# Linear attention with keys and queries in turns, values last, elu split between ScalarE and one VectorE instruction, and the first low-part split on GpSimd

## The chip, the cores and the metric

The kernel runs on one core of one Trainium2 chip. The metric is the device time of the whole program in microseconds. A core has TensorE (PE), VectorE (DVE), ScalarE (ACT), GpSimd (POOL), a queue that issues most transfers (SP) and 16 DMA engines.

## The reference, cut to what matters

Two layers of a perceiver-like network on x of shape (2, 128, 512): each a cross attention, an attention and a feed-forward block. The change is in the second layer's attention and at the start of its feed-forward:

```python
x = x + _L1_attn_ref(_layernorm(x), ...)      # linear attention
x = x + _L1_ffn_ref(_layernorm(x), ...)       # gated, two hidden layers of 2048
# _L1_attn_ref
fmap = lambda t: jax.nn.elu(t) + 1.0
Q = fmap(x @ Wq + bq);  K = fmap(x @ Wk + bk);  value = x @ Wv + bv
KV = jnp.sum(K * value, axis=1);  Ksum = jnp.sum(K, axis=1)
Z = 1.0 / (Q * Ksum[:, None, :] + 1e-06)
V = Q * KV[:, None, :] * Z
out = jax.nn.gelu(V @ Wo + bo)
```

## The kernel before

The program is written engine by engine: `linear_pe`, `linear_act`, `linear_dve` are what TensorE, ScalarE and VectorE do in linear attention, `ffn_pe`, `ffn_scalar`, `ffn_dve` the same for the feed-forward. Each engine takes its instructions in the order in which they are written; between engines stand semaphores, and `link` makes VectorE wait for its own last instruction, `link_a` ScalarE. No planner reorders anything.

T = 256 is both batches' 128 positions side by side, and C = 4 is the number of chunks of 128 of the width 512. Projections are in fp32 and leave `[128 columns of the width, 256 positions]` in PSUM, four accumulated matmuls for a column chunk; they read the normalised, transposed input `xnT`. Weights come in blocks of 128x2048 (1 MB) through a ring of four buffers: block k goes into buffer k % 4, and SP issues it when `blk_used` says that block k - 4 is used up. The blocks of linear attention are K, V, Q and the output projection, in that order in memory; the first feed-forward block takes the buffer of K.

Before: TensorE projects keys, values and queries, one matrix after the other (L2063). VectorE adds the bias to each piece into `lz` (L2095 for keys and values, L2113 for queries), takes the minimum with 0 (L2099, L2114), ScalarE takes the exponential (L2078, L2081), and VectorE adds max(lz, 0) (L2101, L2122). Sums over a batch's positions are reductions (L2103, L2106). For queries it goes on chunk by chunk: denominators (L2126), their reciprocal (L2128), the product `lvT` (L2131), and `lv_ready` lets TensorE do two output matmuls of 512 columns (L2070). Then bias (L2138), gelu on ScalarE (L2085), residual (L2142), statistics for the next layer normalisation (L244 to L252).

The feed-forward multiplies in three passes of a faster number format: each operand is split into a high part, which ScalarE makes by a cast (`split_hi`, L2181; `norm_hi` for the input), and a low part, which VectorE makes by subtracting (`split_lo`, L2186; L2282 for the input). `w_hi` and `w_lo` count split weight blocks. TensorE starts when block 0 and both parts of the input are there (L2215). Where TensorE has to wait it does filler matmuls, `keep_clock` (L279).

GpSimd makes one low part in the first layer (L2401, 128x1024), issues the transfers of the context, and is free after 1050 us.

Of the kernel before, what the change touches and what calls it, by code (L numbers as in the profile page):

```python
# [16 lines left out]
P = 128  # L17
B = 2
D = 512
C = D // P  # L20
T = B * P
# [12 lines left out]
RING = 4  # L34
# [7 lines left out]
BLK_LIN = BLK_X1 + 2  # L42
# [73 lines left out]
def build(nc, x, ctxT, ctx_rows, wq, wk, wv, wo, stream, small, cols, rows, consts, out):  # L116
# [6 lines left out]
    with ExitStack() as ctx:  # L123
# [1911 lines left out]
        lz = view(0, 3, C, T)  # L2035
# [3 lines left out]
        lden = view(8 * C * T, C * B, P)  # L2039
# [5 lines left out]
        LIN_Q_BANK = (2, 3, 4, 5)  # L2045
        lin_filled = sem("lin_filled")
        lmin_ready = sem("lmin_ready")
        lexp_ready = sem("lexp_ready")
        lv_ready = sem("lv_ready")
# [3 lines left out]
        def linear_pe(pe):  # L2053

            norm_pe(pe, 4)
            for m in range(3):
                need(pe, BLK_LIN + m)
                for cc in range(C):
                    out = psum[:, LIN_Q_BANK[cc], 0:T] if m == 2 else psum[:, 4 + 2 * m + cc // 2, (cc % 2) * T:(cc % 2) * T + T]
                    if m == 2 and cc == 2:  # L2060
                        pe.wait_ge(lexp_ready, 1)
                    for c in range(C):
                        last = nc.tensor.matmul(out, block(BLK_LIN + m)[:, c, cc * P:(cc + 1) * P], xnT[:, c, :],  # L2063
                                                start=c == 0, stop=c == C - 1)
                    last.then_inc(lin_filled if cc < C - 1 else blk_used, 1)
            need(pe, BLK_LIN + 3)
            for c in range(C):
                pe.wait_ge(lv_ready, c + 1)
                for b in range(B):
                    last = nc.tensor.matmul(psum[:, b, :], lvT[:, c, b * P:(b + 1) * P], block(BLK_LIN + 3)[:, c, :],  # L2070
                                            start=c == 0, stop=c == C - 1)
                    if c == C - 1:
                        last.then_inc(lin_filled if b == 0 else blk_used, 1)

        def linear_act(act):
            norm_act(act, 4)
            act.wait_ge(lmin_ready, 1)
            nc.scalar.activation(le[:, 0, :, :], le[:, 0, :, :], ACT.Exp).then_inc(lexp_ready, 1)  # L2078
            for cc in range(C):
                act.wait_ge(lmin_ready, cc + 2)  # L2080
                nc.scalar.activation(le[:, 1, cc, :], le[:, 1, cc, :], ACT.Exp).then_inc(lexp_ready, 1)  # L2081
# [5 lines left out]
        def linear_dve(dve):  # L2087
            norm_dve(dve, 4)
            for m in range(2):
                for cc in range(C):  # L2090
# [422 lines left out]
```

## Time and profile before

| | |
|---|---|
| median of 3 runs | 1392.0 us (1389.58, 1392.0, 1392.38) |
| profiled execution | 1391.61 us, span 1389.8 us |
| TensorE busy, mean granted clock | 1319.1 us (95%), 0.978 |
| weight loads busy | 1127.0 us (81%) |
| VectorE busy | 901.5 us (65%) |
| ScalarE busy | 684.6 us (49%) |
| GpSimd busy | 12.0 us (1%) |
| chain that ended last | PE 84%, DVE 10%, issue 3%, ACT 2%, DMA 1% |

The span is the time from the first to the last instruction; the profiled execution's own time is 1.8 us more. Busy shares are of the span. The chain names, at each moment, the work for which everything after it had to wait; an engine's busy time outside the chain costs nothing. A PE row in a timeline counts two records for an fp32 matmul.

### The profile page before, as it was taken

What the parts mean: (1) busy time and instruction counts of PE and PEld (TensorE: products, weight loads), DVE (VectorE), ACT (ScalarE), POOL (GpSimd) and SP (SyncE); (2) the same over time, 40 slices, a digit from 0 to 9 for tenths busy, and PEclk for the clock granted to TensorE, in tenths of its full rate; (3) what the DMA queues carried; (4) which work ended last, traced back from release to release, by engine and by line L of the source; (5) the groups of instructions that cost most, each with busy time, mean ns of one, the idle gap of its engine ahead of it and who ended that gap; (6) DMA issues with size and microseconds to landing.
All of it is one profiled execution on the core that took longest, in us unless ns stands there. A gap on an engine that the chain in (4) does not pass through costs nothing.

```text
span 1389.8 us, 23595 instructions
## 1 busy us (share of the span) xinstructions
PE 1319.1 (95%) x9874; PEld 1127.0 (81%) x9874; DVE 901.5 (65%) x1163; ACT 684.6 (49%) x815; POOL 12.0 (1%) x18
## 2 busy tenths in 40 slices
PE   7999999989999999896899999999899889999998
PEld 6899899979999997665677777777654679999997
DVE  3666565766665666687678888888616667444443
ACT  4534444454444443561377777777404144555442
POOL 0000000000000000000000000000100000000000
PEclk9999999999999999985899999999999999999999
DMA  7101011301010021210079998999840325455552
GB/s 281 40 23 44 20 35 54 127 15 43 20 35 20 21 76 47 92 62 33 31 277 338 342 345 338 343 346 355 331 170 8 121 91 182 172 184 183 185 182 77
DMA packets 50220, 197.67 MB, mean 142 GB/s; under 512 B 12112, under 2 KB 20560, under 8 KB 30416
## 3 DMA queue, kind: packets, MB, share of 16 engines
q1 hardware_dynamic: 47792, 187.41, 37.3%
q0 software_dynamic: 2336, 8.91, 1.9%
q8 instruction: 72, 1.18, 0.3%
q14 instruction: 20, 0.16, 0.0%
HBM read 195.78 MB, written 0.52 MB: 141 GB/s over the span
## 4 chain that ended last, share of the span: by engine, by line
PE 84%; DVE 10%; issue 3%; ACT 2%; DMA 1%; SPq 0%; POOL 0%; POOLq 0%; DVEq 0%; ACTq 0%
PE psum L453 13%; PE psum L2233 13%; PE psum L428 13%; PE psum L1538 8%; PE psum L480 5%; PE psum L1558 4%; PE psum L505 4%; PE psum L1541 4%; PE psum L2215 3%; PE psum L1561 2%; PE psum L2246 2%; PE psum L2063 1%; PE psum L464 1%; PE psum L1570 1%; PE psum L1837 1%
## 5 line engine op out<-in xcount | busy, mean ns | idle before, releaser
L1599 DVE TENSOR_TENSOR arena_r<-ring,arena_r 128x2048 fp32r<-128x2048 f32 x96 | 219.6, 2290 | 36.4 <-ACT arena_r L1593 36.1
L453 PE MATMUL psum<-ring_r,arena_r 128*128 128x256 f32 x1536 | 201.4, 289 | 3.5 <-ACT arena_r L723 2.5
L453 PEld LDWEIGHTS psum<-ring_r,arena_r 128*128 128x128 f32 x1536 | 192.0, 194 | 4.2 <-issue 2.7
L428 PE MATMUL psum<-arena_r 128*128 128x512 f32 x768 | 186.0, 397 | 9.8 <-ACT arena_r L757 9.6
L1593 ACT CAST arena_r<-ring 128x2048 fp32r<-128x2048 f32 x96 | 183.4, 1913 | 17.1 <-PE psum L1541 10.7
L2233 PE MATMUL psum<-arena_r 128*128 128x256 f32 x1536 | 184.6, 283 | 1.1 <-DVE arena_r L2292 1.1
L2233 PEld LDWEIGHTS psum<-arena_r 128*128 128x128 f32 x1536 | 184.4, 192 | 1.3 <-issue 1.3
L428 PEld LDWEIGHTS psum<-arena_r 128*128 128x128 f32 x768 | 143.1, 190 | 42.1 <-issue 8.4
L2186 DVE TENSOR_TENSOR arena_r<-ring,arena_r 128x2048 fp32r<-128x2048 f32 x44 | 100.8, 2292 | 117.0 <-ACT arena_r L2181 117.0
L2181 ACT CAST arena_r<-ring 128x2048 fp32r<-128x2048 f32 x44 | 83.6, 1901 | 111.2 <-PE psum L2233 85.3
L1538 PE MATMUL psum<-arena_r 128*128 128x512 f32 x512 | 132.5, 401 | 1.3 <-issue 1.3
L1538 PEld LDWEIGHTS psum<-arena_r 128*128 128x128 f32 x512 | 94.2, 188 | 23.2 <-issue 5.0
L744 ACT COPY arena<-psum 128x1024 f32<-128x1024 f32 x64 | 61.7, 1016 | 89.6 <-PE psum L480 89.6
L616 DVE TENSOR_TENSOR arena<-arena,psum 128x1024 f32<-128x1024 f32 x64 | 75.2, 1216 | 28.0 <-PE psum L494 28.0
L301 DVE TENSOR_TENSOR arena_r<-arena,arena_r 128x768 fp32r<-128x768 f32 (+2 forms) x25 | 33.7, 1353 | 74.9 <-ACT arena_r L715 57.1
L736 ACT COPY ring<-psum 128x512 f32<-128x512 f32 x64 | 37.3, 582 | 87.0 <-PE psum L453 87.0
L751 ACT ACTIVATE arena<-arena 128x1024 f32<-128x1024 f32 x64 | 66.2, 1058 | 19.8 <-DVE arena L616 18.5
L596 DVE TENSOR_TENSOR arena<-arena 128x512 f32<-128x512 f32 (+1 forms) x128 | 71.5, 559 | 4.4
L1541 PE MATMUL psum<-arena_r 128*128 128x512 f32 x256 | 68.6, 390 | 0.0
L480 PEld LDWEIGHTS psum<-qT,arena 64*128 64x128 f32 x1024 | 59.7, 188 | 9.9 <-issue 9.1
L480 PE MATMUL psum<-qT,arena 64*128 64x128 f32 x1024 | 65.8, 278 | 0.8 <-issue 0.8
L1558 PE MATMUL psum<-arena_r 128*128 128x512 f32 x256 | 64.2, 393 | 0.5 <-DVE arena_r L1767 0.5
(314 smaller groups left out, 1686.3 us busy)
## 6 DMA issues: line engine op xcount, KB each, us to landing
ring<-in_stream SPq DMA_DIRECT2D x151, 1024.0 KB, 4.8
arena<-in_ctxT POOLq DMA_DIRECT2D x8, 1024.0 KB, 11.9
arena<-in_ctxT SPq DMA_DIRECT2D x7, 1024.0 KB, 8.0
arena<-in_wk SPq DMA_DIRECT2D x16, 256.0 KB, 3.2
wv_in<-in_wv SPq DMA_DIRECT2D x8, 512.0 KB, 3.4
arena<-in_wq SPq DMA_DIRECT2D x16, 256.0 KB, 2.6
arena<-in_wk SPq DMA_DIRECT2D x16, 128.0 KB, 3.1
arena<-in_wo SPq DMA_DIRECT2D x2, 1024.0 KB, 6.3
```

Of the source, the lines that this page charges most:

```text
L428: last = nc.tensor.matmul(bank, wk_sb[wp][:, c, w], cx[xp][kb][:, c, :], start=c == wp == xp == 0, stop=c == C - 1 and xp == 1)
L453: last = nc.tensor.matmul(bank[:, q * T:(q + 1) * T], cx[xp][kc // 4][:, c, kc % 4 * P:(kc % 4 + 1) * P], wv_sb[wp][:, c, :], start=c == w ...
L480: last = nc.tensor.matmul(psum[:, 2 * half + kc // 4, kc % 4 * P:kc % 4 * P + P], kT[j % 2][a:a + 64, k0:k0 + P], qT[a:a + 64, j % 2, half ...
L616: nc.vector.tensor_tensor(part, part, per_row(psum[:, SPREAD_BANK, 0:P], KC // 2), ALU.subtract).then_inc(shifted, 1)
L1538: nc.tensor.matmul(out, xg[xp][:, c, e, :], hi[:, c, :], start=c == xp == 0, stop=False)
L1541: last = nc.tensor.matmul(out, xg[0][:, c, e, :], lo[:, c, :], start=False, stop=c == C - 1)
L1558: nc.tensor.matmul(psum[:, 5, :], hT[u][hp][:, f, :], hi[:, f, :], start=u == f == hp == 0, stop=False)
L1593: nc.scalar.copy(mwhi[p % MB], ring[k % RING][:, :]).then_inc(moe_hi, 1)
L1599: nc.vector.tensor_tensor(mwlo[p % MB], ring[(BLK_MOE + p) % RING][:, :], mwhi[p % MB].bitcast(fp32), ALU.subtract).then_inc(moe_lo if p < ...
L2181: nc.scalar.copy(whi[j % 2], ring[k % RING][:, :]).then_inc(w_hi, 1)
L2186: nc.vector.tensor_tensor(wlo[j % 2], ring[(BLK_W12 + j) % RING][:, :], whi[j % 2].bitcast(fp32), ALU.subtract).then_inc(w_lo, 1)
L2233: last = nc.tensor.matmul(psum[:, 4 + s, 0:T], w[wp][:, c, :], src[xp][:, c, :], start=c == wp == xp == 0, stop=c == FC - 1 and wp == 1)
```

## The change

It does these things:

- Keys and queries are projected in turns, piece by piece, and values last; each piece has a PSUM bank of its own, and V takes the banks of K (`lk_ready` says that VectorE has read one).
- 1 + elu(z + b) is written as max(z + b + 1, exp(-relu(-(z + b)))). ScalarE does the relu out of PSUM (L2097) and the exponential (L2099), VectorE one instruction (L2114), which for keys also gives the sum over positions as its accumulator output (`lks`). Key times value is one instruction with `lkvs` as accumulator output (L2135). The bias constants `lone` and `lneg` are made ahead of the layer normalisation.
- Denominators and reciprocals of all chunks come before the values.
- The low part of the first feed-forward block is made by GpSimd; the split of the second comes behind the input's parts on ScalarE and VectorE.
- The residual of batch 0 no longer waits behind a split, and its statistics come right behind it.
- The first buffers of the ring are given free by the first matmul of a later matrix; the count of `blk_used` stays the same at the end.
- Filler ahead of the feed-forward is 10 and 3 matmuls instead of 13 and 4.

```diff
-        def norm_stats_dve(dve, n):
-            for b in range(B):
+        def norm_stats_dve(dve, n, batches=range(B)):
+            for b in batches:
                 ins = nc.vector.bn_stats(stats[:, b, :], x_res[:, b, :])
...
+        LIN_BLK = {"k": BLK_LIN, "v": BLK_LIN + 1, "q": BLK_LIN + 2}
+        LIN_BANK = {"k": (4, 5, 6, 7), "v": (4, 5, 6, 7), "q": (2, 3, 0, 1)}
+        LIN_BIAS = {"k": 0, "v": C, "q": 2 * C}
...
         def linear_pe(pe):
 
             norm_pe(pe, 4)
...
+            def project(m, cc, first_done=0):
+                for c in range(C):
+                    last = nc.tensor.matmul(psum[:, LIN_BANK[m][cc], 0:T], block(LIN_BLK[m])[:, c, cc * P:(cc + 1) * P], xnT[:, c, :],
+                                            start=c == 0, stop=c == C - 1)
+                    if c == 0 and first_done:
+                        last.then_inc(blk_used, first_done)
+                last.then_inc(lin_filled, 1)
+
+            need(pe, LIN_BLK["k"])
+            need(pe, LIN_BLK["q"])
+            for cc in range(C):
+                project("k", cc)
+                project("q", cc)
+            need(pe, LIN_BLK["v"])
+            for cc in range(C):
+                pe.wait_ge(lk_ready, cc + 1)
+                project("v", cc, 1 if cc == 0 else 0)
             need(pe, BLK_LIN + 3)
             for c in range(C):
                 pe.wait_ge(lv_ready, c + 1)
                 for b in range(B):
-                    last = nc.tensor.matmul(psum[:, b, :], lvT[:, c, b * P:(b + 1) * P], block(BLK_LIN + 3)[:, c, :],
+                    last = nc.tensor.matmul(psum[:, 2 + b, :], lvT[:, c, b * P:(b + 1) * P], block(BLK_LIN + 3)[:, c, :],
                                             start=c == 0, stop=c == C - 1)
+                    if c == b == 0:
+                        last.then_inc(blk_used, 2)
...
         def linear_act(act):
             norm_act(act, 4)
...
+            for n in range(2 * C):
+                cc, i, m = n // 2, n % 2, "kq"[n % 2]
+                act.wait_ge(lin_filled, n + 1)
+                col_ = LIN_BIAS[m] + cc
+                link_a(act, nc.scalar.activation(le[:, i, cc, :], psum[:, LIN_BANK[m][cc], 0:T], ACT.Relu,
+                                                 bias=lneg[:, col_:col_ + 1], scale=-1.0))
+                nc.scalar.activation(le[:, i, cc, :], le[:, i, cc, :], ACT.Exp, scale=-1.0).then_inc(lexp_ready, 1)
             split_hi(act, 0)
...
         def linear_dve(dve):
+            nc.vector.tensor_scalar(lone[:, :], K_("lin_b", 0, 3 * C), 1.0, None, ALU.add)
+            link(dve, nc.vector.tensor_scalar(lneg[:, :], K_("lin_b", 0, 3 * C), -1.0, None, ALU.mult))
             norm_dve(dve, 4)
+            halves = [slice(b * P, (b + 1) * P) for b in range(B)]
+            def one_plus_elu(m, cc, t, **kw):
+                i, col_ = "kq".index(m), LIN_BIAS[m] + cc
+                return nc.vector.scalar_tensor_tensor(lqk[:, i, cc, t], psum[:, LIN_BANK[m][cc], t], lone[:, col_:col_ + 1],
+                                                      le[:, i, cc, t], ALU.add, ALU.max, **kw)
+            for cc in range(C):
+                dve.wait_ge(lexp_ready, 2 * cc + 1)
+                for b, t in enumerate(halves):
+                    ins = one_plus_elu("k", cc, t, accum_out=lks[:, cc * B + b:cc * B + b + 1])
+                ins.then_inc(lk_ready, 1)
+                dve.wait_ge(lexp_ready, 2 * cc + 2)
+                link(dve, one_plus_elu("q", cc, slice(0, T)))
+                for b, t in enumerate(halves):
+                    i = cc * B + b
+                    ins = nc.vector.tensor_scalar(lden[:, cc, t], lqk[:, 1, cc, t], lks[:, i:i + 1], 1e-6, ALU.mult, ALU.add)
                 link(dve, ins)
...
+                ins = nc.vector.reciprocal(lden[:, cc, :], lden[:, cc, :])
+            link(dve, ins)
             for cc in range(C):
...
+                dve.wait_ge(lin_filled, 2 * C + cc + 1)
+                col_ = LIN_BIAS["v"] + cc
+                for b, t in enumerate(halves):
+                    i = cc * B + b
+                    ins = nc.vector.scalar_tensor_tensor(lkv[:, i, :], psum[:, LIN_BANK["v"][cc], t], K_("lin_b", col_), lqk[:, 0, cc, t],
+                                                         ALU.add, ALU.mult, accum_out=lkvs[:, i:i + 1])
                 link(dve, ins)
...
+                    ins = nc.vector.scalar_tensor_tensor(lvT[:, cc, t], lqk[:, 1, cc, t], lkvs[:, i:i + 1], lden[:, cc, t],
+                                                         ALU.mult, ALU.mult)
                 ins.then_inc(lv_ready, 1)
...
-            split_lo(dve, 0)
             for b in range(B):
                 dve.wait_ge(lgelu, b + 1)
-                ins = nc.vector.tensor_tensor(x_res[:, b, :], x_res[:, b, :], ly[:, b, :], ALU.add)
-            link(dve, ins)
+                link(dve, nc.vector.tensor_tensor(x_res[:, b, :], x_res[:, b, :], ly[:, b, :], ALU.add))
+                if b == 0:
+                    nc.vector.bn_stats(stats[:, b, :], x_res[:, b, :])
...
         def ffn_pe(pe):
-            keep_clock(pe, 6, 13)
+            keep_clock(pe, 6, 10)
...
-            keep_clock(pe, 6, 4)
+            keep_clock(pe, 6, 3)
...
         def ffn_scalar(act):
             norm_std_act(act, 5)
-            split_hi(act, 1)
             for b in range(B):
                 act.wait_ge(xnT_filled, 2 * 5 + b + 1)
                 nc.scalar.copy(fxT[0][:, :, b * P:(b + 1) * P], psum[:, b, :].rearrange("p (c t) -> p c t", c=C)).then_inc(norm_hi, 1)
+            split_hi(act, 1)
...
         def ffn_dve(dve):
-            norm_stats_dve(dve, 5)
-            split_lo(dve, 1)
+            norm_stats_dve(dve, 5, (1,))
...
+            dve.wait_ge(w_lo, 1)
+            split_lo(dve, 1)
...
+            gp.wait_ge(w_hi, 1)
+            nc.gpsimd.tensor_tensor(wlo[0], ring[BLK_W12 % RING][:, :], whi[0].bitcast(fp32), ALU.subtract).then_inc(w_lo, 1)
```

On ScalarE, at the start of linear attention behind the transposed input's copy (`xnT`), the order is now as follows; `arena` is the memory of `le`:

```order
 L273 COPY xnT<-psum 128x4x128 [waits xnT_filled]
-L2078 ACT_TABLE_LOAD
-L2078 ACTIVATE arena<-arena 128x1024 [waits lmin_ready]
-L2081 ACTIVATE arena<-arena 128x256 [waits lmin_ready] x4
-L2181 CAST arena_r<-ring 128x2048 [waits blk_arrived3]
-L2085 ACT_TABLE_LOAD
-L2085 ACTIVATE arena<-arena 128x512 [waits ly_ready] x2
+L2097 ACTIVATE arena<-psum,lneg 128x256 [waits lin_filled]
+L2099 ACT_TABLE_LOAD
+L2099 ACTIVATE arena<-arena 128x256 [waits a_chain]
+L2097 ACTIVATE arena<-psum,lneg 128x256 [waits lin_filled]
+L2099 ACTIVATE arena<-arena 128x256 [waits a_chain]
```

The exponential's table load has moved from in front of all activations to behind the first relu, and each piece now has two activations of 256 columns.

On VectorE, at the values, one chunk of the program after the change is this (`arena` holds `lkv`, `lqk`, `lden` and `lvT`):

```order
+L2135 SCALAR_TENSOR_TENSOR arena,lkvs<-psum,col,arena 128x128 [waits lin_filled]
+L2135 SCALAR_TENSOR_TENSOR arena,lkvs<-psum,col,arena 128x128
+L2140 SCALAR_TENSOR_TENSOR arena<-arena,lkvs 128x128 [waits v_chain]
+L2140 SCALAR_TENSOR_TENSOR arena<-arena,lkvs 128x128
+L2148 TENSOR_TENSOR arena<-psum,row 128x512 [waits lin_filled]
+L2148 TENSOR_TENSOR arena<-psum,row 128x512 [waits blk_used]
+L2151 TENSOR_TENSOR x_res<-x_res,arena 128x512 [waits lgelu]
+L2153 BN_STATS stats<-x_res 128x6 [waits v_chain]
+L2151 TENSOR_TENSOR x_res<-x_res,arena 128x512 [waits lgelu]
 L244 BN_STATS stats<-x_res 128x6 [waits v_chain]
```

Between an output projection's chunk and the one before it stand now four short instructions, no reciprocal; and between the bias additions (L2148) and the residual (L2151) no split any more.

On GpSimd, at the end of its program:

```order
+L2419 DMA arena<-in_ctxT 128x4x512 x5
+L2422 DMA arena<-in_ctx_rows,pick 128x512 [waits picked] x2
+L2425 TENSOR_TENSOR arena_r<-ring,arena_r 128x2048 [waits w_hi]
 L123 UNCONDITIONAL_BRANCH
```

The subtraction is its last instruction and waits for ScalarE's high part alone.

## Rows read from the trace of the kernel before

**Rows 1.** Windows, linear attention's second half; busy us (instructions) of each engine, clock, DMA

```profile
1104.30:1119.10 14.80, 7.96 (x18) 3.09 (x18) 12.99 (x27) 4.04 (x5) 0.00 (x0) 1.00 0.21 71
```

**Rows 2.** Chain that ended last, 1060 to 1150: start us, us, what

```profile
1083.36 17.52 PE psum L2063 x80
...
1103.29 1.76 DVE arena L2128
```

**Rows 3.** Timeline of PE: start us, us, line, what, count, idle before

```profile
1083.36 20.96 PE L2063 MATMUL psum<-xnT,ring 128*128 128x256 f32 x96 [0.72 <-DVE xnT L261]
1105.84 1.95 PE L2070 MATMUL psum<-ring,arena 128*128 128x512 f32 x4 [1.53 <-DVE arena L2131]
...
1117.07 1.98 PE L2070 MATMUL psum<-ring,arena 128*128 128x512 f32 x4 [1.31 <-DVE arena L2131]
1118.89 5.78 PE L279 MATMUL psum<-cst 128*128 128x256 f32 x26
1125.96 1.11 PE L2199 MATMUL psum<-cst,xn 128*128 128x128 f32 x8 [1.29 <-DVE xn L252]
...
1130.54 46.30 PE L2215 MATMUL psum<-arena_r 128*128 128x256 f32 x384 [1.74 <-issue]
```

**Rows 4.** Timeline of DVE, 1068 to 1150

```profile
1102.77 0.48 DVE L2126 TENSOR_SCALAR arena<-arena,lks 128x128 f32<-128x128 f32 x2
...
1105.08 0.61 DVE L2131 SCALAR_TENSOR_TENSOR arena<-arena,lkvs 128x128 f32<-128x128 f32 x2
...
1119.09 0.69 DVE L2138 TENSOR_TENSOR arena<-psum,row 128x512 f32<-128x512 f32 x1 [0.17 <-PE psum L2070]
1119.70 2.28 DVE L2186 TENSOR_TENSOR arena_r<-ring,arena_r 128x2048 fp32r<-128x2048 f32 x1
1121.90 1.29 DVE L2142 TENSOR_TENSOR x_res<-x_res,arena 128x512 f32<-128x512 f32 x2
1123.22 1.29 DVE L244 BATCH_NORM_STATS2 stats<-x_res 128x6 f32<-128x512 f32 x2
...
1126.94 2.29 DVE L2186 TENSOR_TENSOR arena_r<-ring,arena_r 128x2048 fp32r<-128x2048 f32 x1 [0.58 <-ACT arena_r L2181]
1129.15 1.28 DVE L2282 TENSOR_TENSOR arena_r<-psum,arena_r 128x512 fp32r<-128x512 f32 x2
```

**Rows 5.** Timeline of ACT, 1068 to 1150

```profile
1083.27 1.28 ACT L2078 ACT_TABLE_LOAD   x1
...
1101.72 0.42 ACT L2081 ACTIVATE arena<-arena 128x256 f32<-128x256 f32 x1 [8.48 <-DVE arena L2114]
...
1110.79 1.88 ACT L2181 CAST arena_r<-ring 128x2048 fp32r<-128x2048 f32 x1
...
1119.82 0.63 ACT L2085 ACTIVATE arena<-arena 128x512 f32<-128x512 f32 x1 [0.23 <-DVE arena L2138]
```

**Rows 6.** Groups of instructions by line: busy us, mean ns of one, idle before

```profile
L2289 DVE SCALAR_TENSOR_TENSOR arena<-psum,col,arena 128x256 f32<-128x256 f32 x16 | 7.7, 478 | 3.7 <-ACT arena L2262 3.7
...
L2262 ACT ACTIVATE arena<-psum,col 128x256 f32<-128x256 f32 x16 | 7.5, 470 | 8.4 <-PE psum L2215 8.4
```

**Rows 7.** Timeline of ACT in the second cross attention, accumulator reads

```profile
1050.45 0.19 ACT L1941 ACTIVATION_READ_ACCUMULATOR arena<-psum,nlm 128x1 f32 x1
1050.54 0.36 ACT L1941 ACTIVATE arena<-psum,nlm 128x128 f32<-128x128 f32 x1
```

**Rows 8.** Timeline of all engines, 681.7 to 686

```profile
681.78 2.41 POOL L2401 TENSOR_TENSOR arena_r<-xn,arena_r 128x1024 fp32r<-128x1024 f32 x1 [112.17 <-ACT arena_r L1607]
...
683.43 0.80 DVE L1664 TENSOR_TENSOR gt_rank<-sc,gm 128x16 f32<-128x16 f32 x1
...
685.30 0.18 DVE L1664 TENSOR_TENSOR gt_rank<-gt_rest,gm 128x16 f32<-128x16 f32 x1
```

**Rows 9.** DMA issues of L222 between 1085 and 1100

```profile
DMA to landing us min/median/max: 4.8/4.8/4.9
```

**Rows 10.** Windows, 630 to 642, columns as in rows 1

```profile
630.00:642.00 12.00, 4.64 (x72) 4.08 (x76) 11.04 (x17) 1.58 (x4) 0.00 (x0) 0.55 0.18 72
```

More of the change, by code:

```diff
@@ L2032, in cross1_dve @@
             link(dve, nc.vector.tensor_tensor(x_res[:, 1, :], x_res[:, 1, :], psum[:, X1_BANK[1], :], ALU.add))
-        lz = view(0, 3, C, T)
         le = view(3 * C * T, 2, C, T)
@@ L2038, in build @@
         lkv = view(7 * C * T, C * B, P)
-        lden = view(8 * C * T, C * B, P)
+        lden = view(8 * C * T, C, T)
         lvT = view(9 * C * T, C, T)
@@ L2043, in build @@
         lks = sb("lks", [P, C * B])
-        LIN_Q_BANK = (2, 3, 4, 5)
+        lneg = sb("lneg", [P, 3 * C])
+        lone = sb("lone", [P, 3 * C])
+        LIN_BLK = {"k": BLK_LIN, "v": BLK_LIN + 1, "q": BLK_LIN + 2}
+        LIN_BANK = {"k": (4, 5, 6, 7), "v": (4, 5, 6, 7), "q": (2, 3, 0, 1)}
+        LIN_BIAS = {"k": 0, "v": C, "q": 2 * C}
         lin_filled = sem("lin_filled")
-        lmin_ready = sem("lmin_ready")
         lexp_ready = sem("lexp_ready")
+        lk_ready = sem("lk_ready")
         lv_ready = sem("lv_ready")
@@ L2055, in linear_pe @@
             norm_pe(pe, 4)
[L2056 to L2065, printed above, removed]
+            def project(m, cc, first_done=0):
[14 more added lines that the diff above has]
+                project("v", cc, 1 if cc == 0 else 0)
             need(pe, BLK_LIN + 3)
@@ L2116, in linear_dve @@
-            query_in(0)
-            for cc in range(C):
-                if cc + 1 < C:
-                    query_in(cc + 1)
-                dve.wait_ge(lexp_ready, cc + 2)
-                q = lqk[:, 1, cc, :]
-                link(dve, nc.vector.scalar_tensor_tensor(q, lz[:, 2, cc, :], 0.0, le[:, 1, cc, :], ALU.max, ALU.add))
-                den = lden.rearrange("p (c b) t -> p c (b t)", c=C)[:, cc, :]
-                for b in range(B):
-                    i, t = cc * B + b, slice(b * P, (b + 1) * P)
-                    ins = nc.vector.tensor_scalar(den[:, t], q[:, t], lks[:, i:i + 1], 1e-6, ALU.mult, ALU.add)
+            halves = [slice(b * P, (b + 1) * P) for b in range(B)]
@@ L2129, in linear_dve @@
-                for b in range(B):
-                    i, t = cc * B + b, slice(b * P, (b + 1) * P)
-                    ins = nc.vector.scalar_tensor_tensor(lvT[:, cc, t], q[:, t], lkvs[:, i:i + 1], den[:, t], ALU.mult, ALU.mult)
+                for b, t in enumerate(halves):
+                    i = cc * B + b
+                    ins = nc.vector.scalar_tensor_tensor(lvT[:, cc, t], lqk[:, 1, cc, t], lkvs[:, i:i + 1], lden[:, cc, t],
+                                                         ALU.mult, ALU.mult)
```

34 lines of the change are left out of this document (2 added, 32 removed).

## The prediction

> **What bounds the kernel now.** I read the table of windows first, then the chain of work that ended last, then the timelines of the engines around linear attention. TensorE is busy for 95% of the span (the table above), so an edit pays only where TensorE has nothing to do, or does filler. Between the last projection and the end of the output projection there is such a place: TensorE is busy 7.96 of 14.80 us, VectorE 12.99 [rows 1]. The chain says who ends last: it runs in TensorE for 17.52 us of projections, and then in VectorE, whose reciprocals of 1.76 us are on it four times [rows 2]. TensorE's timeline shows the same from its side: projections for 20.96 us, then four groups of output matmuls, the first at 1105.84 and the last at 1117.07, with idle time between them; then filler, the transposes at 1125.96, filler, and the first feed-forward matmul at 1130.54 [rows 3]. VectorE's timeline fills the last stretch [rows 4]: after the second bias addition (1119.09) a low-part split of 2.28 us, only then the residual (1121.90) and the statistics, later a second split of 2.29 us in front of the two low parts of the normalised input (1129.15), whose end at 1130.43 releases the feed-forward. From 1130.54 on nothing in the chain is touched by the change. So two stretches can be won: the projections to the end of the output projection, and from there to 1130.54.
>
> I count t from the first projection matmul (1083.36). Before, the last output group starts at t = 33.7 and ends at about 35.7; the feed-forward starts at 47.2.
>
> **Ahead of t = 0.** `lone` and `lneg` stand between the residual and the statistics. They are two tiny instructions, and the statistics wait for the second; the smallest two-input instruction takes 0.18 us [rows 8], so the pair is between 0.2 and 0.4. I take 0.3 us, lost: nothing hides it.
>
> **Projections.** Twelve of them take 20.96 us, 1.73 each once the drain of the last is left out. The order becomes k q k q k q k q v v v v, with the same work. K and Q are done at t = 13.9, V at 20.8 if no wait for `lk_ready` bites.
>
> ScalarE per piece: one activation out of PSUM, 0.47 [rows 6], an estimated 0.13 for the wait between the two (0.05 to 0.3 changes nothing), and an exponential of 0.42 [rows 5], 1.02 together, against 1.73 between pieces, so it keeps up. The table load of 1.28 that was hidden in idle time [rows 5] now stands behind the first relu; the first pair is late by it (keys at 4.2, queries at 5.1), and it is never repeated.
>
> VectorE per column chunk: two halves of 1+elu for keys, one whole for queries 0.48 [rows 6], two denominators 0.48, a reciprocal 1.75 [rows 2, 4]. The keys' halves carry an accumulator output, which no instruction of VectorE has before. Bounds: without it a pair out of SBUF takes 0.61 [rows 4], some 0.68 out of PSUM; on ScalarE the accumulator read starts the next instruction 0.09 later [rows 7]; at worst each read costs as much as a smallest instruction on its own, 0.2 to 0.3. I take 0.88 a pair, as its nearest relative on ScalarE says, range 0.68 to 1.3. A chunk is then 0.88+0.51+0.52+1.75 = 3.6, against 3.46 of two projections: nearly balanced. From 5.1 for the first query: first reciprocal done at 8.0, the fourth at 18.8. `lk_ready` comes at 5.1, 8.8, 12.5 and 16.1, always ahead of V's need (13.9, 15.6, 17.3, 19.1).
>
> Values: an accumulating pair (0.9) and the scaled pair (0.61), 1.5 per chunk: `lv_ready` at 20.3, 21.8, 23.3, 24.7. The output projection has the columns of four projections, so unhindered it goes 20.8 to 27.7, and wants them at 20.8, 22.5, 24.3 and 26.0. TensorE would bound it: 8.0 us earlier than before's 35.7.
>
> **GpSimd's split.** The buffer of the K block is now given free at V's first matmul, t = 14.4, instead of about 7.0. A block lands 4.8 us after its issue [rows 9], with 0.4 for the queue: 19.6. ScalarE's half takes 1.88 [rows 5], to 21.5. GpSimd then subtracts 2048 columns. Its one row with half of them says 2.41, so 4.8: 21.6 to 26.4. That is far ahead of the feed-forward's need. But it isn't free. During the 2.41 us of GpSimd's subtraction before, VectorE's L1664 with two SBUF inputs took 0.80 us, ending just when GpSimd was done (684.23 against 684.19); the same instruction 1.9 us later takes 0.18 [rows 8]. So VectorE's instructions with two SBUF inputs stand still until GpSimd ends. Those are the scaled pairs (`lqk`, `lden`). The second one ends at 21.8, about when GpSimd starts; I take it that it slips through. The third, due at 22.7, is held to 26.4: `lv_ready` 3 at 27.0 instead of 23.3. TensorE, which wanted it at 24.3, loses 2.8; the fourth comes at 28.5, in time for 28.8. The output projection ends at 30.5: 5.2 earlier than before, not 8.0.
>
> The Trainium skill, in SBUF — State Buffer, "Who interferes with whom", states it as a lock: a VectorE instruction with two SBUF inputs and a GpSimd one that reads SBUF exclude each other, for a whole instruction. The trace agrees with its 0.80 against 0.18. By its GPSIMD Engine Reference, "3.1 Elementwise", a 2048-column fp32 addition is 4.50 us on GpSimd; by that figure the loss would be an estimated 2.5.
>
> **From there to the feed-forward.** The split of 2.28 leaves VectorE. The second gelu ends at 1120.45 [rows 5]; the residual of batch 0 starts behind the second bias addition, at 1119.8 in old time, its statistics, the other residual and its statistics follow: four times 0.65 to 0.7, to 1122.5, where it was 1124.51 [rows 4]. Saved 2.0. Then the second split: ScalarE copies the transposed input first (0.58 each), VectorE subtracts behind each copy and no longer behind 2.29 of split. The chain is transposes, copy, subtract 0.68 for batch 1: the feed-forward starts 1.95 sooner still. Together 3.95. The split of block 1 lies behind, beside the first 48 feed-forward matmuls, 5.8 us (46.30 for 384) [rows 3]: 1.88 and 2.29 one after the other end 3.6 us after its start. If that cover were gone it would cost up to 4.2. The filler, 10 and 3 instead of 13 and 4, shrinks by 1.8 and stays shorter than the waits that it fills; it costs nothing.
>
> **The sum.** −5.2 + 0.3 − 3.95 = −8.85. The profiled execution took 1391.61, so 1382.8; the median of the runs shown is 0.4 above it, so 1383.0. What a measurement of this kernel tells from no change is about 0.2%, 2.8 us.
>
> **The rivals.**
> *No collision* (26%): GpSimd starts later or shorter than I think, or an operand in PSUM leaves the interface free. Speaks for it: half a microsecond decides. Sum −8.0+0.3−3.95 = −11.65: 1380.1.
> *The collision one chunk sooner* (17%): GpSimd gets in between the halves of the second scaled pair. `lv_ready` 2 at 27.0 against 22.5: 4.5 lost instead of 2.8, 1384.8.
> *Accumulating is dear* (8%): 1.3 a pair makes a chunk 4.1, so the fourth reciprocal ends at 20.2, the first scaled pair already meets GpSimd, and `lv_ready` is 1.95 apart from 27.0 on: the end at 34.6, 1387.2. The Trainium skill, in ScalarE: Activation LUTs, "Rules for kernel authors", would keep relu on VectorE; here that would put another 0.48 a piece on the engine that the chain runs in, and no run here shows it.
> *The split on the wrong side of the clock* (2%), the slower one: TensorE waits 2.8 us for the third scaled pair with no filler. In another stretch, where it was busy 4.64 of 12 us, the granted clock fell to 0.55 [rows 10], between its two levels 1.2 and 2.4 GHz. At 1.2 GHz the busy time doubles. To lose the 8.85 and 2.8 more it takes 23 us at the lower level. Against it: gaps of 1.53 and 1.31 us and two more ahead of these same matmuls left the clock at 1.00 [rows 1, 3]. Over 1395.
> *The change is hidden* (2%): something else, a late block 1 say, holds the feed-forward; about 1390.
> My forecast has 45%.
>
> **The numbers.** 1383.0. No collision and 1384.8 are inside; a dearer accumulator reaches 1386.5, and with the spread of the runs the lower bound is 1379.3. Faster 0.95, same 0.03, slower 0.02.
>
> **What would show it.** A table load once, behind the first relu. TensorE without gaps over the twelve projections. The output projection's first matmul 20.8 us after the first projection's. A scaled pair on VectorE of over 3 us that ends with GpSimd's instruction, and as long a gap in TensorE. The feed-forward 7.5 us after the output projection's end, where it was 11.5. Wrong would make it: `lk_ready` as what V waits for, a w_hi or w_lo wait of TensorE at the third pair of feed-forward columns, or a granted clock under 1.00 between t = 20 and 50.

## The result, and the profile after

The changed kernel takes 1378.91 us, the median of 6 runs (1376.2 to 1383.62), against 1390.0 for the kernel before (6 runs, 1387.96 to 1392.38). The ratio is 0.9907, with a 95% interval of 0.9888 to 0.9926. Measured a second time it is 0.9916 (0.9889 to 0.9943). It is faster, by a little less than 1%, and both intervals leave out 1. 1383.0 was predicted, with 1379.3 to 1386.5 as the range: the gain is larger than forecast, and the first median lies 0.4 us below the range. The second, 1379.71 from 10 runs, lies inside it, so what was wrong has to be read from the trace and not from the whole time.

The head of the page of the changed kernel:

```profile
span 1375.0 us, 23605 instructions
...
PE 1313.6 (96%) x9866; PEld 1123.1 (82%) x9866; DVE 896.1 (65%) x1175; ACT 688.9 (50%) x826; POOL 16.5 (1%) x19
```

The spans of the two profiled executions differ by 14.8 us, but that is not the change alone. What runs before t = 0 is the same code but for the 0.3 us of `lone` and `lneg`, and it took 1083.36 us in one execution and 1079.79 in the other. In the thirteen profiles of this study the first projection matmul starts between 1079.79 and 1090.05. So I compare from there on, in t, as the prediction did. The timeline of PE, which answers to [rows 3]:

```profile
1079.79 20.96 PE L2065 MATMUL psum<-xnT,ring 128*128 128x256 f32 x96 [0.72 <-DVE xnT L261]
1100.59 5.31 PE L2084 MATMUL psum<-ring,arena 128*128 128x512 f32 x12
1106.15 1.98 PE L2084 MATMUL psum<-ring,arena 128*128 128x512 f32 x4 [0.26 <-DVE arena L2140]
...
1112.96 1.11 PE L2209 MATMUL psum<-cst,xn 128*128 128x128 f32 x8 [0.51 <-DVE xn L252]
...
1115.66 46.31 PE L2225 MATMUL psum<-arena_r 128*128 128x256 f32 x384 [0.29 <-issue]
```

Three groups of output matmuls are one row now, without a gap; the fourth waits for 0.26 us for a scaled pair (L2140). The output projection ends at t = 28.3 (35.7 before), the feed-forward starts at t = 35.87 (47.18 before). The residual of batch 1 starts 5.57 us ahead of t = 0 instead of 5.30. Together −11.31 + 0.27 = −11.04 us.

The timeline of DVE, which answers to [rows 4]. First the second half of a key pair beside the read of the first half, and the chunk's reciprocal, then the last reciprocal, values and scaled pairs, then the tail:

```profile
1090.88 0.08 DVE L2114 DVE_READ_ACCUMULATOR arena<-psum,lone,arena 128x1 f32 x1
1090.88 0.35 DVE L2114 SCALAR_TENSOR_TENSOR arena<-psum,lone,arena 128x128 f32<-128x128 f32 x1
...
1092.42 1.75 DVE L2128 RECIPROCAL arena<-arena 128x256 f32<-128x256 f32 x1
...
1095.87 1.75 DVE L2128 RECIPROCAL arena<-arena 128x256 f32<-128x256 f32 x1
1097.66 0.35 DVE L2135 SCALAR_TENSOR_TENSOR arena<-psum,col,arena 128x128 f32<-128x128 f32 x1
...
1098.33 0.61 DVE L2140 SCALAR_TENSOR_TENSOR arena<-arena,lkvs 128x128 f32<-128x128 f32 x2
...
1100.71 0.61 DVE L2140 SCALAR_TENSOR_TENSOR arena<-arena,lkvs 128x128 f32<-128x128 f32 x2
1101.24 0.35 DVE L2135 SCALAR_TENSOR_TENSOR arena<-psum,col,arena 128x128 f32<-128x128 f32 x1
...
1101.90 4.20 DVE L2140 SCALAR_TENSOR_TENSOR arena<-arena,lkvs 128x128 f32<-128x128 f32 x2
...
1108.78 0.68 DVE L2151 TENSOR_TENSOR x_res<-x_res,arena 128x512 f32<-128x512 f32 x1
1109.50 0.69 DVE L2153 BATCH_NORM_STATS2 stats<-x_res 128x6 f32<-128x512 f32 x1
1110.11 0.68 DVE L2151 TENSOR_TENSOR x_res<-x_res,arena 128x512 f32<-128x512 f32 x1
1110.82 0.69 DVE L244 BATCH_NORM_STATS2 stats<-x_res 128x6 f32<-128x512 f32 x1
...
1114.27 1.29 DVE L2291 TENSOR_TENSOR arena_r<-psum,arena_r 128x512 fp32r<-128x512 f32 x2 [0.91 <-ACT arena_r L2265]
```

The first three scaled pairs take 0.61 us each, the third (1100.71) with GpSimd's instruction starting 0.46 us after it (1101.17, below), and the last one takes 4.20. The accumulator read is a record of its own (0.08), and the second half starts in the same moment as the read of the first. The residual and the statistics follow the bias addition with nothing between. The timeline of ACT:

```profile
1081.79 0.47 ACT L2097 ACTIVATE arena<-psum,lneg 128x256 f32<-128x256 f32 x1 [2.10 <-PE psum L2065]
1082.29 1.28 ACT L2099 ACT_TABLE_LOAD   x1
...
1090.43 0.47 ACT L2097 ACTIVATE arena<-psum,lneg 128x256 f32<-128x256 f32 x1 [0.80 <-PE psum L2065]
1090.93 0.42 ACT L2099 ACTIVATE arena<-arena 128x256 f32<-128x256 f32 x1
...
1099.19 1.90 ACT L2191 CAST arena_r<-ring 128x2048 fp32r<-128x2048 f32 x1 [4.39 <-DMA ring<-in_stream]
```

Timeline of POOL, the same kernel:

```profile
1101.17 4.52 POOL L2425 TENSOR_TENSOR arena_r<-ring,arena_r 128x2048 fp32r<-128x2048 f32 x1 [53.45 <-ACT arena_r L2191]
```

One table load, behind the first relu; a piece takes ScalarE 0.92 us (1090.43 to 1091.35). ScalarE's half of the split ends at t = 21.3, GpSimd subtracts from 21.4 to 25.9, and the long pair runs from 22.1 to 26.3. The chain of work that ended last, at the same place:

```profile
1079.79 14.07 PE psum L2065 x64
...
1101.90 4.21 DVE arena L2140 x2
```

### The profile page after: what moved, and what is told of

Its sections match the earlier page's. It is cut to its first block, busy times and chain, and to the rows that moved or that the text cites. A ratio compares the mean times of both kernels' runs of the same rounds, so it can differ in the third digit from the quotient of the medians.

```text
span 1375.0 us, 23605 instructions
## 1 busy us (share of the span) xinstructions
PE 1313.6 (96%) x9866; PEld 1123.1 (82%) x9866; DVE 896.1 (65%) x1175; ACT 688.9 (50%) x826; POOL 16.5 (1%) x19
## 4 chain that ended last, share of the span: by engine, by line
PE 86%; DVE 9%; ACT 2%; DMA 2%; issue 1%; SPq 0%; DVEq 0%; ACTq 0%
PE psum L2243 13%; PE psum L453 13%; PE psum L428 13%; PE psum L1538 8%; PE psum L480 5%; PE psum L1558 4%; PE psum L505 4%; PE psum L1541 4%; PE psum L2225 3%; PE psum L1561 2%; PE psum L2256 2%; PE psum L1837 2%; PE psum L464 1%; PE psum L1570 1%; PE psum L2065 1%
```

## The experiments

All were read in t, from the first projection matmul, because the stages ahead of it vary by more than the effects. What every profile gave, one execution each:

| kernel | t = 0 is at | output projection ends, t | feed-forward starts, t |
|---|---|---|---|
| before | 1083.36 | 35.69 | 47.18 |
| changed | 1079.79 | 28.34 | 35.87 |
| GpSimd's split alone | 1085.73 | 39.64 | 49.18 |
| split of block 1 behind, alone | 1090.05 | 35.69 | 45.30 |
| linear attention alone | 1082.18 | 27.83 | 39.31 |
| changed, profiled a second time | 1083.94 | 28.35 | 35.88 |
| changed, GpSimd after the pairs | 1082.38 | 27.82 | 35.35 |
| changed, GpSimd 1.7 us sooner | 1088.30 | 30.01 | 37.54 |
| the same, in four instructions | 1083.48 | 28.70 | 36.22 |
| changed, values 1.2 us later | 1083.08 | 30.13 | 37.66 |
| changed, no accumulator output | 1084.71 | 28.68 | 36.21 |
| changed, no filler | 1084.39 | 28.35 | 36.60 |
| changed, GpSimd after the pairs, constants early | 1083.53 | 27.83 | 35.35 |

The changed kernel's two profiles agree within 0.01 us in both columns, though their t = 0 lie 4.15 us apart. Five of the versions were timed once only: GpSimd sooner 1386.93 us, in four instructions 1380.82, values later 1381.83, no accumulator output 1382.01, no filler 1383.87. Runs of one kernel lie up to 14 us apart here (17 runs of the kernel before: 1386.16 to 1400.63), so these five times show nothing by themselves, and only the stage in the trace is read.

**My theory** was the prediction's own: the terms add up, GpSimd's instruction holds VectorE's instructions with two SBUF inputs, and only the place where it meets them was wrong. **The rival**: the long pair has another cause, GpSimd costs nothing, and the miss is in another term.

**GpSimd's split alone**, on the kernel before:

```diff
-            split_lo(dve, 0)                     # linear_dve
+            dve.wait_ge(w_lo, 1)                 # ffn_dve, ahead of split_lo(dve, 1)
+            gp.wait_ge(w_hi, 1)
+            nc.gpsimd.tensor_tensor(wlo[0], ring[BLK_W12 % RING][:, :], whi[0].bitcast(fp32), ALU.subtract).then_inc(w_lo, 1)
```

> The kernel before with one edit: the low part of the first feed-forward block is made by GpSimd, nothing else. Counted from the first projection matmul, the last output group starts at 33.7 us and the feed-forward at 47.2 us in the kernel before. Lock theory (a VectorE instruction with two SBUF inputs stands still while GpSimd subtracts): ScalarE's half ends where it ended before, GpSimd subtracts for 4.5 us from about 29.3 on, the third scaled pair (0.61 us) becomes a wait of over 3 us, the last output group starts at about 37.3, and the split of 2.3 us that leaves the path later does not pay for it: feed-forward at about 48.6, 1.4 us later than before. Rival (the long pair in the changed kernel had another cause, GpSimd is free): last group at 33.7, feed-forward at 45.0, 2.2 us earlier.

Timeline of DVE, the same kernel:

```profile
1115.47 4.55 DVE L2131 SCALAR_TENSOR_TENSOR arena<-arena,lkvs 128x128 f32<-128x128 f32 x2
```

Timeline of POOL, the same kernel:

```profile
1115.12 4.49 POOL L2414 TENSOR_TENSOR arena_r<-ring,arena_r 128x2048 fp32r<-128x2048 f32 x1 [62.90 <-ACT arena_r L2180]
```

Timeline of PE, the same kernel:

```profile
1120.08 5.29 PE L2070 MATMUL psum<-ring,arena 128*128 128x512 f32 x8 [5.07 <-DVE arena L2131]
...
1134.91 46.30 PE L2214 MATMUL psum<-arena_r 128*128 128x256 f32 x384 [1.32 <-issue]
```

The same pair that took 0.61 us takes 4.55 as soon as GpSimd subtracts beside it, and TensorE waits 5.07 us for it, where it waited 2.03 for that pair before. The feed-forward starts 2.0 us later than before, although a split of 2.3 us has left VectorE. In time: 1393.21 against 1391.04, ratio 1.0012 (0.999 to 1.0035), which is no difference that a measurement of whole times can tell; the trace can. The lock theory had it at 48.6, it is 49.18; the rival said 45.0. A side effect is seen in the windows (length, busy us of the engines, granted clock, DMA):

```profile
1113.00:1115.00 2.00, 2.00 (x3) 0.34 (x1) 1.93 (x4) 2.00 (x2) 0.00 (x0) 0.52 0.00 0
...
1123.00:1125.00 2.00, 2.00 (x6) 0.89 (x5) 0.76 (x3) 0.00 (x0) 0.00 (x0) 0.92 0.00 0
```

The clock was at its lower level already before the long wait, at output matmuls that ran at 1.00 in the kernel before with the same gaps ahead of them, and it stayed there until 1123. In the output projection this cost next to nothing: the last output group ends 2.67 us after its scaled pair starts (1122.70 to 1125.37), and did so 2.65 us after it in the kernel before (1116.40 to 1119.05). So the wait for the held pair is what ends the output projection 3.95 us later (t = 39.64 instead of 35.69), and 1.95 of it come back behind it, where the split of 2.3 us is gone.

**The split of block 1 behind the input's parts, alone**, on the kernel before:

```diff
             norm_std_act(act, 5)                 # ffn_scalar
-            split_hi(act, 1)
             for b in range(B): ...               # the input's high parts
+            split_hi(act, 1)
-            split_lo(dve, 1)                     # ffn_dve, the same
             for b in range(B): ...
+            split_lo(dve, 1)
```

> The kernel before with one edit: the split of the second feed-forward block comes behind the input's parts on ScalarE and VectorE. My sum's term: last output group unchanged at 33.7, feed-forward at 45.2 instead of 47.2. Rival (block 1 is then late for the third pair of feed-forward columns): the same start, but a gap in TensorE some 5.8 us behind it, and no gain in all.

Timeline of PE, the same kernel:

```profile
1135.35 46.30 PE L2215 MATMUL psum<-arena_r 128*128 128x256 f32 x384
```

Feed-forward at t = 45.30, 1.88 sooner (1.95 predicted), and its 384 matmuls take the same 46.30 us as in [rows 3]: block 1 is not late. In time the ratio is 1.0001 (0.9983 to 1.002): 1.88 us are 0.14%, inside that interval.

**Linear attention alone**, on the changed kernel:

```diff
-            gp.wait_ge(w_hi, 1)
-            nc.gpsimd.tensor_tensor(wlo[0], ...)
+            split_lo(dve, 0)                     # linear_dve, as before
                                                  # residual, statistics, split of block 1, filler: as before
```

> The changed linear attention alone: both splits, the residual, the statistics and the filler are as in the kernel before, and GpSimd does nothing here. The terms add up: last output group at 26.0 us from the first projection matmul (33.7 before, 26.4 in the changed kernel with GpSimd's collision), feed-forward 13.5 later at 39.5: some 7.4 us of the changed kernel's 11. Rival (linear attention's part is worth less by itself, because the tail needs the early buffers): feed-forward later than 40.5.

Timeline of PE, the same kernel:

```profile
1102.98 7.03 PE L2084 MATMUL psum<-ring,arena 128*128 128x512 f32 x16
```

All sixteen records of the output projection are one row of 7.03 us: without GpSimd TensorE never waits there. It ends at 27.83, 7.86 us sooner than before, and the feed-forward starts 7.87 sooner. In time 1384.14, ratio 0.995 (0.9931 to 0.997): −6.9 us between the medians, where the trace has −7.87 + 0.27.

**GpSimd after the scaled pairs**, on the changed kernel:

```diff
+            gp.wait_ge(lv_ready, C)
             gp.wait_ge(w_hi, 1)
```

> The changed kernel with one edit: GpSimd also waits until all four scaled pairs are done. Lock theory: the fourth scaled pair takes 0.6 us instead of 4.2 and ends at 22.8 us; the last output group starts at 26.0 instead of 26.4, so 0.3 us are won and no more, because TensorE is the bound there; GpSimd ends at 27.4, before VectorE's residual, and the feed-forward starts at 35.5 instead of 35.9. Rival (the pair is long for another reason): it stays at 4.2.

Timeline of DVE, the same kernel:

```profile
1104.49 0.61 DVE L2140 SCALAR_TENSOR_TENSOR arena<-arena,lkvs 128x128 f32<-128x128 f32 x2
```

Timeline of POOL, the same kernel:

```profile
1105.20 4.51 POOL L2426 TENSOR_TENSOR arena_r<-ring,arena_r 128x2048 fp32r<-128x2048 f32 x1 [54.93 <-DVE arena L2140]
```

The fourth pair is back at 0.61 us, and the feed-forward starts at 35.35: the collision cost the changed kernel 0.5 us. I had said 0.3 to 0.4. In time 1377.85, ratio 0.9913 (0.9891 to 0.9935), not to be told from the changed kernel.

**GpSimd 1.7 us sooner**, on the changed kernel:

```diff
-                project("q", cc)
+                project("q", cc, 1 if cc == C - 1 else 0)
...
-                project("v", cc, 1 if cc == 0 else 0)
+                project("v", cc)
```

> The changed kernel with one edit: the buffer of the K block is given free by the first matmul of the last query piece, 1.7 us sooner. Everything that GpSimd does is then 1.7 us sooner: 19.7 to 24.2 us from the first projection matmul. Lock theory: the second scaled pair, which starts at 19.7, or the third at 20.9 is held until 24.2. If the second: lv_ready 2 at 24.6 where TensorE wants it at 22.5, 2.0 us lost, last output group at 28.0 instead of 26.4. If the third: lv_ready 3 at 24.8, wanted at 24.3, 0.5 lost, last group at 26.5. A collision one chunk sooner is then dearer although nothing else changed. Rival (no lock): last group at 26.4 or 26.0 and no long pair at the place where GpSimd works.

Timeline of DVE, the same kernel:

```profile
1108.03 4.81 DVE L2140 SCALAR_TENSOR_TENSOR arena<-arena,lkvs 128x128 f32<-128x128 f32 x2
```

Timeline of POOL, the same kernel:

```profile
1107.93 4.50 POOL L2425 TENSOR_TENSOR arena_r<-ring,arena_r 128x2048 fp32r<-128x2048 f32 x1 [51.93 <-ACT arena_r L2191]
```

Timeline of PE, the same kernel:

```profile
1112.89 5.42 PE L2084 MATMUL psum<-ring,arena 128*128 128x512 f32 x12 [1.92 <-DVE arena L2140]
```

GpSimd had begun 0.1 us before the second pair's turn, and that pair takes 4.81 us; the second output group starts at t = 24.59, where I had put 24.6. TensorE waits 1.92 us, and the feed-forward starts at 37.54, 1.67 later than in the changed kernel. By its trace, a buffer that is free sooner made this stage slower.

**The same in four instructions**, so that VectorE may get a turn in between:

```diff
-            nc.gpsimd.tensor_tensor(wlo[0], ring[BLK_W12 % RING][:, :], whi[0].bitcast(fp32), ALU.subtract).then_inc(w_lo, 1)
+            for h in range(4):
+                s = slice(h * BLK // 4, (h + 1) * BLK // 4)
+                ins = nc.gpsimd.tensor_tensor(wlo[0][:, s], ring[BLK_W12 % RING][:, s], whi[0][:, s].bitcast(fp32), ALU.subtract)
+            ins.then_inc(w_lo, 1)
```

> As the run with the earlier buffer, and GpSimd subtracts in four instructions of 512 columns instead of one of 2048. If the interface is held for a whole instruction and then given up, a held pair waits for at most a quarter, some 1.2 us, and VectorE and GpSimd take turns: no pair over 2 us, last output group at 26.0 to 26.3. If VectorE stands still as long as GpSimd has anything to do, the picture is that of the run with one instruction.

Timeline of DVE, the same kernel:

```profile
1103.21 2.66 DVE L2140 SCALAR_TENSOR_TENSOR arena<-arena,lkvs 128x128 f32<-128x128 f32 x2
...
1106.45 1.97 DVE L2140 SCALAR_TENSOR_TENSOR arena<-arena,lkvs 128x128 f32<-128x128 f32 x2
```

Timeline of POOL, the same kernel:

```profile
1103.19 5.08 POOL L2427 TENSOR_TENSOR arena_r<-ring,arena_r 128x512 fp32r<-128x512 f32 x4 [52.00 <-ACT arena_r L2191]
```

The first half of the second pair by itself (the other takes 1.35):

```profile
1103.21 1.39 DVE L2140 SCALAR_TENSOR_TENSOR arena<-arena,lkvs 128x128 f32<-128x128 f32 x1
```

The two engines take turns, instruction by instruction: a quarter on GpSimd (some 1.3 us), half a pair, the next quarter, the other half. Two pairs are held, by 2.05 and 1.36 us, instead of one by 4.2. My "no pair over 2 us" was wrong, since a pair is two instructions and each can meet a quarter of its own. The last output group starts at 26.7, not at 26.0 to 26.3. The feed-forward starts at 36.22 instead of 37.54: most of the loss is gone, and 0.9 us against the version without a collision are left.

**Values 1.2 us later**, on the changed kernel:

```diff
             link(dve, ins)                       # the reciprocals
+            link(dve, nc.vector.reduce_sum(lkvs[:, 0:C], lqk[:, 0, :, :], AX.X))
```

> The changed kernel with one more reduction of 1.2 us on VectorE (one SBUF input, its result is overwritten) between the reciprocals and the values. It sets VectorE about as late as my prediction had it, with GpSimd where it was: 21.4 to 25.9 us from the first projection matmul. My prediction's price for the third scaled pair, redone with the measured 1.2 a chunk: the pair that was due at 22.1 is held to 25.9, lv_ready 3 at 26.5 where TensorE wants it at 24.3, last output group at 28.3 instead of 26.4, feed-forward at 37.8 instead of 35.9: 1.9 lost to a delay of 1.2. If instead the loss is VectorE's delay alone: the last group's wait grows from 0.26 to at most 1.5, last group below 27.6.

Timeline of DVE, the same kernel:

```profile
1105.26 4.20 DVE L2141 SCALAR_TENSOR_TENSOR arena<-arena,lkvs 128x128 f32<-128x128 f32 x2
```

Timeline of PE, the same kernel:

```profile
1109.51 3.70 PE L2084 MATMUL psum<-ring,arena 128*128 128x512 f32 x8 [2.04 <-DVE arena L2141]
```

This is the case of my prediction, made on purpose: the third pair is the long one, TensorE waits 2.04 us, and the feed-forward starts at 37.66 (37.8 expected), 1.8 us later for 1.2 us of work. Against the version without a collision (35.35) the third pair's collision costs 2.3 us, where I had 2.8 with longer chunks.

**No accumulator output**, on the changed kernel (the sums over positions are left out and stand at 1.0):

```diff
+            nc.vector.memset(lks[:, :], 1.0)
+            nc.vector.memset(lkvs[:, :], 1.0)
-                    ins = one_plus_elu("k", cc, t, accum_out=lks[:, cc * B + b:cc * B + b + 1])
+                    ins = one_plus_elu("k", cc, t)
...
-                                                         ALU.add, ALU.mult, accum_out=lkvs[:, i:i + 1])
+                                                         ALU.add, ALU.mult)
```

> The changed kernel without the two accumulator outputs: the sums over positions of keys and of keys times values are left out and stand at 1.0, so the output is another one. It measures what accumulating costs. As the trace of the changed kernel reads (the accumulator read of 0.08 us lies beside the next instruction): nothing, the key pair stays at 0.55 to 0.6 us and the last reciprocal ends at the same 17.8 us. As my prediction had it: each read 0.1, so the pair would fall by 0.2 to 0.3 and the value chunks by as much, four of them ending 1 us earlier.

Timeline of DVE, the same kernel:

```profile
1100.79 1.75 DVE L2130 RECIPROCAL arena<-arena 128x256 f32<-128x256 f32 x1
1102.58 0.61 DVE L2137 SCALAR_TENSOR_TENSOR arena<-psum,col,arena 128x128 f32<-128x128 f32 x2
...
1103.75 0.61 DVE L2137 SCALAR_TENSOR_TENSOR arena<-psum,col,arena 128x128 f32<-128x128 f32 x2
...
1106.73 4.62 DVE L2142 SCALAR_TENSOR_TENSOR arena<-arena,lkvs 128x128 f32<-128x128 f32 x2
```

A value chunk takes 1.17 us (1102.58 to 1103.75) where it takes 1.19 with the sums. The last reciprocal ends at t = 17.83 in both, which tells little, because TensorE sets the pace there; from the start of the first reciprocal to that of the second, where VectorE never waits, it is 3.12 us without the sums and 3.15 with them. So the accumulator read costs 0.02 to 0.03 us a chunk. The feed-forward starts 0.34 us later, not sooner: in this execution the transfer of the block takes 5.1 us instead of 4.7, so ScalarE's half starts at t = 19.74 instead of 19.40 and GpSimd at 21.7 instead of 21.4, and the fourth pair is held for longer (4.62). Why the transfer took longer stays open.

**No filler** ahead of the feed-forward, on the changed kernel:

```diff
-            keep_clock(pe, 6, 10)
...
-            keep_clock(pe, 6, 3)
```

> The changed kernel without the filler matmuls between the output projection and the feed-forward (10 and 3). My prediction: filler only fills waits and costs nothing, so the feed-forward starts at the same 35.9 us. What it tells is the clock: TensorE is then idle for about 5 us ahead of the transposes. If its clock falls, the first matmuls of the feed-forward run at 1.2 GHz for some us, and the feed-forward takes 1.5 to 2 us longer; if not, it is the same.

Timeline of PE, the same kernel:

```profile
1117.57 1.97 PE L2208 MATMUL psum<-cst,xn 128*128 128x128 f32 x8 [4.83 <-DVE xn L252]
1120.99 48.08 PE L2223 MATMUL psum<-arena_r 128*128 128x256 f32 x384 [1.45 <-ACT arena_r L2263]
```

Windows, the same kernel (length, busy us of PE, PEld, DVE, ACT, POOL, granted clock, DMA):

```profile
1122.00:1124.00 2.00, 2.00 (x11) 2.00 (x11) 1.94 (x1) 1.26 (x1) 0.00 (x0) 0.50 0.00 0
...
1126.00:1128.00 2.00, 2.00 (x19) 2.00 (x19) 1.20 (x3) 0.39 (x1) 0.00 (x0) 1.00 0.00 0
```

After 4.83 us without a matmul the clock is at 0.50, which is 1.2 GHz, and back at 1.00 only 5 us into the feed-forward. The transposes take 1.97 us instead of 1.11, the 384 matmuls 48.08 instead of 46.31, and the feed-forward starts at 36.60, 0.73 later, where I had expected the same 35.9: 2.5 us lost. In the changed kernel with its filler the gap is 0.51 us, and the clock stays at 1.00 in its window, from t = 0 to the feed-forward:

```profile
1079.80:1115.70 35.90, 34.85 (x147) 26.81 (x147) 27.73 (x69) 16.37 (x26) 4.52 (x1) 1.00 0.31 117
```

**GpSimd after the pairs, and the constants early**, beside the changed kernel once more:

```diff
+            nc.vector.tensor_scalar(lone[:, :], ...)             # cross1_dve, ahead of
+            link(dve, nc.vector.tensor_scalar(lneg[:, :], ...))  # dve.wait_ge(x1_proj, 2)
...
-            nc.vector.tensor_scalar(lone[:, :], ...)             # the same two at
-            link(dve, nc.vector.tensor_scalar(lneg[:, :], ...))  # the start of linear_dve
...
+            gp.wait_ge(lv_ready, C)
```

> The changed kernel with two edits: GpSimd waits for the four scaled pairs, and lone and lneg are made while VectorE waits for the last output matmuls of the cross attention. My theory: 0.3 us less between the residual and the first projection matmul, 0.5 less from there to the feed-forward (35.35 instead of 35.9), 0.8 together, which is 0.06% and below what the times can tell; they should stand between 0.989 and 0.993 of the kernel before. If the constants were free anyway, the distance from the residual's start to the first projection matmul stays at 5.6 us instead of 5.3.

> The changed kernel once more, beside the version with two edits: 11.0 us less than before by the two stages of its trace, so a ratio of 0.992. If the first measurement of 11.1 owed much to its small number of runs, 0.990 or 0.994 would come out.

Timeline of DVE, the same kernel:

```profile
1078.24 0.69 DVE L2034 TENSOR_TENSOR x_res<-x_res,psum 128x512 f32<-128x512 f32 x1 [3.78 <-PE psum L1878]
```

Timeline of PE, the same kernel:

```profile
1083.53 20.96 PE L2067 MATMUL psum<-xnT,ring 128*128 128x256 f32 x96 [0.72 <-DVE xnT L261]
...
1118.88 46.31 PE L2225 MATMUL psum<-arena_r 128*128 128x256 f32 x384 [0.29 <-issue]
```

From the residual to the first projection 5.29 us instead of 5.57, from there to the feed-forward 35.35 instead of 35.87: 0.80 us, as expected. In time the two are equal: 1379.87, ratio 0.9915 (0.9884 to 0.9946), and 1379.71, 0.9916, for the changed kernel. By its trace it is 0.8 us ahead; that it is the faster one isn't shown by the times.

## Why the prediction was wrong

**What bounds it**: right. Both stretches were open, and nothing behind the feed-forward's start moved (46.30 and 46.31 us for its 384 matmuls).

**Ahead of t = 0**: 0.3 predicted, 0.27 measured.

**Projections**: right in order and table load. They take 20.96 us without a gap, `lk_ready` is never waited for. ScalarE needs 0.92 a piece where I had 1.02.

**The step that failed: "I take 0.88 a pair, as its nearest relative on ScalarE says", and with it "1.5 per chunk"** of values. The accumulator read lies beside the next instruction: a key pair is done after 0.53 to 0.63, which is below even the lower bound of 0.68, and a value chunk takes 1.19. VectorE therefore was not nearly balanced with TensorE but ahead of it: from its first reciprocal to its second it took 3.15 us where I had 3.6, and from then on the chunks went at the pace of TensorE (the reciprocals of the last two start 3.45 us apart). The last reciprocal ended at 17.8 instead of 18.8, and the third scaled pair began at 20.9, not at 22.7: 1.0 us of these 1.8 from the keys and queries, the rest from the value chunks. Without the hold `lv_ready` would have come at 19.1, 20.3, 21.5 and 22.7.

**GpSimd's split**: the mechanism was right, and it hit the wrong pair. The block landed at 19.4 where I had put 19.6, GpSimd took 4.52 instead of 4.8 and began at 21.4 instead of 21.6. But VectorE had begun its third pair by then (20.9 to 21.5), so the fourth was held, until 26.3, and TensorE wanted it only at 25.8. So the mis-sized term of the sum is the −5.2, and in it the 2.8 for the held pair: it measured 0.5, and the term −7.87 + 0.52 = −7.35. Almost all of the 2.2 us by which −8.85 missed −11.04 is that. What I called the first rival, no collision, comes nearer in time (−11.65) for the wrong reason: there was a collision, and TensorE had its slack there. The run with values later moved it onto the third pair, and the price rose from 0.5 to 2.3.

**The tail**: 3.95 predicted. The run without a collision and the run of linear attention alone differ by it: 35.35 − 39.31 = −3.96, of which 1.88 is the split of block 1 (1.95 predicted) and 2.08 is left for the first split and the residual's order together (2.0 predicted). That remainder is by subtraction; no run took the two apart. The shorter filler cost nothing that shows, since TensorE still waits 0.51 us behind it; no filler would have cost 2.5.

So the −11.04 consist of −7.87 and +0.27 for linear attention, −1.88, −2.08 and +0.52 for the collision.

**The sum's base**: I started from 1392.0, the median of three runs (less 8.85 that is 1383.15; I wrote 1383.0). The six runs of before gave 1390.0, and later sets of 29 and 17 gave 1391.04 and 1390.86. Of the 4.1 us between 1383.0 and 1378.9, 2.2 are the collision's place and the rest is the base, which is the spread of medians of few runs and no property of the kernel. My lower bound allowed for one of the two only; it took no collision as 1380.1 and added 0.8 for the spread of the runs. At the other end the range was not consistent: the rival with dear accumulating came to 1387.2, outside the 1386.5 that was to cover it.

**Left open**: why the stages ahead of t = 0, which were not touched, take 1079.8 to 1090.1 us from execution to execution. It is more than any term here. The whole time goes with the mean granted clock: of 46 runs of the kernel before, the 14 with 0.978 or more average 1388.8 us and the 11 with 0.974 or less 1393.7. How much of the spread ahead of t = 0 is the clock's, no run here shows.

## What to carry to other kernels

Work that is given to GpSimd is not free for VectorE: find which VectorE instructions with two SBUF inputs will lie beside it, and for when the consumer wants their results; the same collision cost 0.5 us on the fourth chunk, 2.3 on the third and 2.2 on the second, against the 2.1 us that the split and the residual's order were worth together. An accumulator output on VectorE cost 0.02 to 0.03 us a chunk here and replaced a reduction (1.22 us for four chunks before). When the whole time varies by more than the effect, count from an event ahead of the change in each trace, and add up the parts there.

## What the runs showed of the hardware that was not expected

- VectorE's accumulator read is a record of 0.08 us that overlaps the next instruction: chunks of 1.19 us with it, 1.17 without. On ScalarE the next instruction begins 0.09 us after the read does [rows 7].
- A VectorE instruction with one input in PSUM and one in SBUF (L2135, from 1101.24 on in the changed kernel) runs at its usual 0.35 us beside GpSimd's subtraction; with both in SBUF a pair is held for up to 4.2 us, at most as long as the one GpSimd instruction (4.50). The Trainium skill has this rule in SBUF — State Buffer, "Who interferes with whom", and the traces agree.
- Between two GpSimd instructions a waiting VectorE instruction gets its turn; four quarters take GpSimd 5.08 us where one instruction takes 4.50.
- After 4.83 us without a matmul the granted clock fell to 0.50. With gaps of 1.3 to 2.0 us between the output groups it stayed at 1.00 in the kernel before and fell in the run with GpSimd's split alone, which is the same code up to there: such gaps alone did not tell which it would be. In the runs with GpSimd sooner and with values later, TensorE waited 1.92 and 2.04 us once, and the clock stayed at 1.00.
